# give_back at step 12, projections one step ahead, and three of the scan's sixteen states beside the filter's tail and the value projections

## What is computed

```python
xn = layernorm(x)
# first layer: a state space filter with further small products, and two experts of eight for each sequence
def step(h, t):                       # the scan, 16 states for each of 256 inner channels
    delta_t, B_t, C_t, u_t = t
    h = exp(delta_t * A) * h + delta_t * B_t * u_t
    return h, einsum('bdn,bn->bd', h, C_t)
x = x + filter(xn) + experts(xn)
xn = layernorm(x)
# second layer: causal attention, 16 heads of 64, and two experts of eight for each token
attn = softmax(where(causal, -inf, q @ k.T) / sqrt(64)) @ v
x = x + attn @ wo.T + bo + token_experts(xn)
```

## Time and profile before

| | us |
|---|---|
| three runs | 2887.19, 2894.98, 2903.43; median 2894.98 |
| the profiled execution | 2911.0 |
| its span, first to last instruction | 2909.2 |
| busy: TensorE | 2210.0 (76%) |
| busy: VectorE | 1641.0 (56%) |
| busy: ScalarE | 1182.3 (41%) |
| busy: GpSimd | 956.3 (33%) |
| mean granted clock of TensorE | 0.856 |

### The profile page before, as it was taken

One profiled execution on the slowest core, in us unless ns is written; L12 is line 12 of the kernel. 1 busy time (PEld: TensorE's weight loads), 2 busy tenths in 40 slices (PEclk: granted clock), 3 DMA queues, 4 the chain that ended last, 5 costly groups with the idle time before them and its releaser, 6 DMA issues.

```text
span 2909.2 us, 38779 instructions
## 1 busy us (share of the span) xinstructions
PE 2210.0 (76%) x11640; PEld 1519.0 (52%) x11640; DVE 1641.0 (56%) x2929; ACT 1182.3 (41%) x2702; POOL 956.3 (33%) x581
## 2 busy tenths in 40 slices
PE   3257878877798777976788777887779877788785
PEld 1033556554565545654456545655556555565564
DVE  2953775456754666546765467545675466644231
ACT  2222653434533454334543345333453345423441
POOL 0320661036510563006620176103641057302401
PEclk8577889987899888887899878998799888989897
DMA  2000012211122111211113111221112211131123
GB/s 89 0 15 5 35 67 65 83 52 34 57 89 83 40 47 48 97 65 33 47 60 109 52 38 66 66 83 52 36 55 90 82 40 47 51 122 55 58 73 123
DMA packets 82452, 175.06 MB, mean 60 GB/s; under 512 B 11448, under 2 KB 42560, under 8 KB 81984
## 3 DMA queue, kind: packets, MB, share of 16 engines
q1 hardware_dynamic: 78144, 164.05, 16.8%
q0 software_dynamic: 4096, 8.40, 1.0%
HBM read 123.71 MB, written 15.14 MB: 48 GB/s over the span
## 4 chain that ended last, share of the span: by engine, by line
PE 47%; issue 21%; DVE 11%; POOL 10%; ACT 9%; DMA 2%; SPq 0%; ACTq 0%; POOLq 0%; DVEq 0%
PE G L895 7%; PE G L999 4%; PE G L1014 4%; PE FM L988 4%; POOL REG L1879 3%; POOL YG L1893 3%; PE G L906 2%; PE G L988 2%; DVE HS L1468 2%; PE G L976 2%; PE G L1031 2%; PE FM L718 2%; POOL Y L1868 2%; ACT REG L1258 2%; PE FM L865 1%
## 5 line engine op out<-in xcount | busy, mean ns | idle before, releaser
L1868 POOL TENSOR_TENSOR Y<-Y,HC 128x1024 f32<-128x1024 f32 x128 | 322.9, 2523 | 340.4 <-DVE HC L1480 340.1
L1279 ACT ACTIVATE REG<-G 128x128 f32<-128x128 f32 (+3 forms) x512 | 222.9, 435 | 517.4 <-PE G L999 514.9
L1879 POOL TENSOR_TENSOR REG<-REG,cos_t 128x512 f32<-128x512 f32 x128 | 223.0, 1743 | 570.0 <-ACT REG L1258 569.0
L1014 PE MATMUL G<-REG 128*128 128x64 f32 x2560 | 378.3, 283 | 0.5 <-DVE REG L1761 0.4
L1014 PEld LDWEIGHTS G<-REG 128*128 128x128 f32 x2560 | 364.9, 211 | 1.1 <-issue 0.9
L1468 DVE TENSOR_TENSOR_SCAN HS<-DA,D 128x1024 f32<-128x1024 f32 x128 | 336.1, 2626 | 12.8
L895 PEld LDWEIGHTS G<-XGT,MW 128*128 128x128 f32 x1920 | 296.5, 239 | 57.6 <-issue 57.5
L895 PE MATMUL G<-XGT,MW 128*128 128x128 f32 x1920 | 304.4, 326 | 18.9 <-DMA MW<-moe 18.9
L988 PE MATMUL G<-REG 64*128 64x128 f32 (+3 forms) x768 | 246.5, 536 | 88.8 <-ACT REG L1258 57.7
L988 PE MATMUL FM<-REG 64*128 64x256 f32 (+1 forms) x256 | 143.9, 648 | 175.3 <-ACT EW L1289 65.1
L999 PE MATMUL G<-ident,REG 128*128 128x128 f32 x1280 | 255.3, 302 | 21.1 <-ACT REG L1279 19.1
(11 more groups left out here) (279 smaller groups left out, 3760.0 us busy)
## 6 DMA issues: line engine op xcount, KB each, us to landing
MW<-moe SPq DMA_DIRECT2D x120, 768.0 KB, 4.3
REG<-ROT SPq DMA_DIRECT2D x256, 128.0 KB
EW<-experts SPq DMA_DIRECT2D x16, 514.5 KB, 4.3
XG<-x_rows SPq DMA_DIRECT2D x8, 960.0 KB, 5.6
y_rows<-YO SPq DMA_DIRECT2D x120, 64.0 KB, 1.5
X<-xT SPq DMA_DIRECT2D x8, 256.0 KB, 5.7
W<-weights SPq DMA_DIRECT2D x1, 2048.0 KB, 9.5
REG<-xT SPq DMA_DIRECT2D x8, 256.0 KB, 3.0
```

The source lines that it names most:

```text
L1014: mm = pe.matmul(G[3][:, col:col + DK], PT[:, n % 2, c * P:(c + 1) * P], V[:, c, j * P + h * DK:j * P + (h + 1) * DK], start=c == 0, stop= ...
L1279: act.activation(PT[:, n % 2, 0:width], G[2][:, 0:width], ACT.Copy).then_inc(pt_copy.sem, 1)
L1868: pool.tensor_tensor(Y[:, :, :], Y[:, :, :], HC[:, n % 2, :, :], ALU.add).then_inc(y_add.sem, 1)
L1879: pool.tensor_tensor(rotated, rotated, cos_t[:, :], ALU.mult).then_inc(rope_d.sem, 1)
```

## The change

Three things move; no computation is added or left out.

1. RETURN_STEP goes from 8 to 12, so give_back stands four steps later on TensorE and VectorE. number_places stays in step 9.
2. Project stands in the step before the one that lends its bank, ahead of weigh_values; rotate comes ahead of the two maxima; on ScalarE add_bias, copy_out and rows_turned come right after the step's first copy_turned.
3. States 0 and 1 of the scan are put into phase 1, between filter steps 23 and 28 (kind "s"). State 0 and 1 use the bank FM for B and the place HC_EARLY in REG for HC. State 2 stands in the value stage. The other 13 states are spread over the 32 steps by the table PIECES, about 2.5 steps each. The norms nf and nx use FB alone, so that FC is free for the row of C.

```diff
+        HC_EARLY = REG[:, 14:16, :]
...
+        EARLY = 2
+        EARLY_AT = {23: ((0, 0),), 24: ((0, 1),), 25: ((0, 2), (1, 0)), 26: ((1, 1),), 27: ((1, 2),)}
...
+            PHASE_1 += [("s", piece) for piece in EARLY_AT.get(p, ())]
...
-        PLACE_AT, NUMBER_AT, RETURN_STEP = 2, 9, 8
+        PLACE_AT, NUMBER_AT, RETURN_STEP = 2, 9, 12
...
+        FIRST = EARLY + 1
+        PIECES = {s_: [] for s_ in range(STEPS)}
+        for n_ in range(FIRST, STATES):
+            at_ = (n_ - FIRST) * STEPS / (STATES - FIRST)
+            for part_ in range(3):
+                PIECES[int(at_ + (0.0, 0.7, 1.7)[part_])].append((n_, part_))
...
+            def early_scan(f, n, part, b):
+                if part == 0:
+                    front_b(f, n, b, FM)
+                elif part == 1:
+                    front_c(f, n, b)
...
                 project(b, 1)
-                values_in(b)
+                if f is not None:
+                    front_b(f, EARLY, b)
+                    front_c(f, EARLY, b)
+                values_in(b, f)
...
+                project(b, 2)
                 for s in range(STEPS):
                     j, t_ = s // TILES, s % TILES
                     key = loan[s][0] if s in loan else (None, None)
-                    if key[0] == "proj":
-                        project(b, key[1])
-                    elif key[0] == "out":
+                    following = loan[s + 1][0] if s + 1 in loan else (None, None)
+                    if key[0] == "out":
                         turn_out(b, key[1])
...
                     turn(b, 2 * s + 1)
                     if t_ == 0 and s + 2 < STEPS:
                         scores(b, s + 2)
+                    if following[0] == "proj":
+                        project(b, following[1])
                     weigh_values(b, 2 * s)
...
+                if n == 0 and f is not None:
+
+                    act.wait_ge(y_add.sem, y_add.at(f, EARLY))
...
                 for s in range(STEPS):
                     copy_turned(b, 2 * s)
-                    if f is not None and s % 2 == 0:
-                        front_step(f, s // 2, (1,))
-                    if s + 1 < STEPS:
-                        exponentials(b, 2 * s + 2)
-                    copy_turned(b, 2 * s + 1)
                     key = loan[s][0] if s in loan else (None, None)
                     if key[0] == "proj":
                         add_bias(b, key[1])
...
                     if s + 1 < STEPS:
-                        exponentials(b, 2 * s + 3)
-                    if f is not None and s % 2 and s // 2 + 1 < STATES:
-                        front_step(f, s // 2 + 1, (0,))
+                        exponentials(b, 2 * s + 2, f)
+                    if f is not None:
+                        for n, part in PIECES[s]:
+                            if part == 0:
+                                front_step(f, n, (0,))
+                    copy_turned(b, 2 * s + 1)
+                    if f is not None:
+                        for n, part in PIECES[s]:
+                            if part == 0:
+                                front_step(f, n, (1,))
+                    if s + 1 < STEPS:
+                        exponentials(b, 2 * s + 3, f)
...
                     key = loan[s][0] if s in loan else (None, None)
+                    if key[0] == "proj":
+                        rotate(b, key[1])
                     if s + 1 < STEPS:
                         largest(b, 2 * s + 2)
                         largest(b, 2 * s + 3)
...
-                        if s % 2:
-                            front_step(f, s // 2, 2)
-                        else:
-                            front_step(f, s // 2, 0)
-                            front_step(f, s // 2, 1)
+                        for n, part in PIECES[s]:
+                            front_step(f, n, part)
...
+                    for n in range(EARLY):
+                        front_step(f, n, True)
...
-                    if f is not None and n % 4 == 3:
-                        front_step(f, n // 4)
+                    if f is not None and n % 2:
+                        for k, part in PIECES[s]:
+                            if part == 2:
+                                front_step(f, k)
```

More of the change, by code:

```diff
@@ L530, in each_step @@
                     front_start(f, k, b)
+                if kind == "s" and f is not None:
+                    early_scan(f, k[0], k[1], b)
         @block.sync
@@ L750, in front_b @@
                     if filtered is not None:
-                        pe.wait_ge(nx.s_root.sem, nx.s_root.at(filtered, 1))
-                pe.matmul(FB[:, :], pick[:, n, :], S3[:, :], start=True, stop=True).then_inc(b_mm.sem, 1)
+                        pe.wait_ge(yf_d.sem, yf_d.at(filtered))
+                if filtered is not None and n == EARLY:
+                    pe.wait_ge(xn2_d.sem, xn2_d.at(filtered))
+                pe.matmul(bank[:, :], pick[:, n, :], S3[:, :], start=True, stop=True).then_inc(b_mm.sem, 1)
             def front_c(b, n, filtered=None):
@@ L945, in values_in @@
                         pe.wait_ge(v_copy.sem, v_copy.at(b, n + 1 - len(V_BANK)))
+                    elif n == 2 and f is not None:
+                        pe.wait_ge(db_mul.sem, db_mul.at(f, EARLY))
                     elif n == 3:
@@ L1790, in phase_2 @@
                         largest(b, 2 * s + 3)
+                    if key[0] == "return" and t is not None:
+                        give_back(t, ring_bank[key])
                     if t_ == 0 and j:
                         divide(b, j - 1)
[L1793 to L1796 removed]
                     if s == 1:
@@ L1867, in front_step @@
                 pool.wait_ge(hc_mul.sem, hc_mul.at(b, n + 1))
-                pool.tensor_tensor(Y[:, :, :], Y[:, :, :], HC[:, n % 2, :, :], ALU.add).then_inc(y_add.sem, 1)
+                pool.tensor_tensor(Y[:, :, :], Y[:, :, :], HC_EARLY if early else HC[:, n % 2, :, :], ALU.add).then_inc(y_add.sem, 1)
             def front_end(b):
```

80 lines of the change are left out of this document (50 added, 30 removed).

## The result

The changed kernel takes 2730.8 us (median of four runs, 2729.52 to 2738.27) against 2891.09 (four runs, 2870.63 to 2903.43): ratio 0.946, 95% interval 0.940 to 0.952. The profiled execution took 2738.3 us against 2911.0, 172.7 less; its span is 2736.5. The medians are 160 us apart: the profiled execution of the kernel before was 20 us slower than its median, that of the changed kernel 8.

The account below looks back on a forecast made before the run. No engine is full; hand-over between engines bounds the kernel. Six full laps at -16.5 us (-99), first -15, last -7 make -121 on the profiled 2911.0: 2790, as a median 2775 us; range 2705 to 2870.

Parts of the forecast that it names:

- more comes back: Rival: 24 us of bank waits go, nothing left at number_places, -28 us a lap, median 2695 us; chance 0.15.
- under 15: Sign: TensorE's waits for ScalarE before scores total under 15 us a lap, from 30.8 before.
- the new wait: Sign: TensorE waits before project about 12 us a lap, 0.9 us at each of 13 projections.
- the tail grew: Sign in the filter's tail: XN2 stands 22 to 23 us after the preceding norm's root, before 18.6.
- 16, 3 and 3.5: Savings forecast for a full lap, in us: new order 16, three states out of the steps 3, later give_back 3.5.
- part 2: Three of sixteen scan states leave the attention steps: 3 us a lap saved there, outer bound 6.7.
- The wait before place_i: Sign: VectorE idles 5 to 10 us before the place_i cast, waiting for GpSimd's sum; TensorE feels about 4.
- part 1: Attention steps: projections one step ahead, ScalarE's bias or copy before the exponential; 16 us a lap saved, bounds 0 and 30.8.
- Part 3: give_back at step 12: TensorE's 7.5 us wait goes, number_places waits instead; net -3.5 us, between 0 and -7.5.
- Scans held up by GpSimd: Rival: each of 13 scans may meet a GpSimd add, 9 us a lap, +65, so 2840 us; chance 0.12.
- Project blocking TensorE: Rival: project waits for late exponentials, 3.3 us each, +75, so 2970 us; decides from 2.5 us a projection; chance 0.08.

Follow-up runs that it names:

- e1: Kernel before the change with only give_back moved, from step 8 to step 12; ratio 0.983, 2851 us.
- e3: Kernel before with only the scan's states moved: two into the filter's tail, one into the value stage, thirteen spread over the steps; ratio 0.969, 2816 us.
- e10: Kernel before with decays and norms re-placed and the last three of sixteen states left out, the other thirteen in the old pairs of steps; ratio 0.988, 2857 us.
- e2: Kernel before with only the new order of projections, rotations and ScalarE's bias and copies; states and give_back as before; ratio 0.982, 2847 us.
- e5: Changed kernel with projections, rotations and ScalarE's bias and copies back in the old order; ratio to the kernel before 0.953, 2763 us.
- e4: Changed kernel with give_back put back to step 8; ratio to the kernel before 0.953, 2763 us.
- e7: Changed kernel with GpSimd's sum of the picked rows moved ahead of the weights of the rows; ratio to the kernel before 0.930, 2695 us.
- e12: Changed kernel with no early states: all sixteen in the steps, D and scan in different steps; ratio to the kernel before 0.954, 2766 us.
- e8: Changed kernel with project at its old place on TensorE, VectorE and ScalarE keeping the new order; ratio to the kernel before 0.935, 2712 us.

## Why the prediction came out as it did

The time, 2731 us, lies in the range (2705 to 2870) and 44 below the forecast, 4 outside the forecast's own band (2735 to 2815); it stands between the forecast and the rival "more comes back" (2695). The terms against the two profiles, the stretches cut at the first and last exponential and at XN2 (rounded):

| | forecast, us | measured |
|---|---|---|
| steps, six full laps | -135 | -164 |
| steps, first lap | -19 | -20 |
| steps, last lap | -7 | -19 |
| phase 1, the tail in it | +26 | +23 |
| value stages | +14 | +9 |
| the rest | 0 | -1 |
| all | -121 | -173 |

**Right: the mechanisms and their places.** Scores no longer wait for lent banks (1.3 us, "under 15"), project has the new wait (14.9, forecast 12), give_back waits for nothing, the sum is waited for before place_i instead, and the tail grew to 22.8 us (forecast 22 to 23). The idle time of the full lap fell by 22.5 us (22.3 in the mean), as 16, 3 and 3.5 make; that it agrees so well is in part luck, as part 2 below shows. The wait before place_i was 3.7 us (5.1 in one of the six laps) where 5 to 10 was expected. The agreement of phase 1 (+26 and +23) is partly luck as well, since its laps come in two lengths, as the last section shows.

**Mis-sized: what a wait is worth.** The terms counted idle time alone. I named the clock (0.84) only in favour of a rival, and gave it no term. Busy time fell by 5.0 us a full lap in the mean, 30 over six, which is the whole difference between -135 and -164; in the last, idle fell by 12.7 where 7 was forecast, and busy by 6.4 more. e1 shows the second at its cleanest: a wait of 6.3 us removed, 13.6 gained in the last lap; in its full laps busy time went the other way.

**Failed: who removes the bank waits.** Part 2 said: "What it costs the steps is the difference of the two laps", and set 3 us a lap with 6.7 as the outer bound; e3 measured 17.4 (mean of six laps, 173.5 to 156.1). A lap with scans against one without tells only what the states' number costs, and that price held: 0.98 a state forecast, 1.2 in e10. It says nothing of a new spacing of the same work. D and scan apart take many of the waits that part 1 had claimed for itself: in e3, without part 1, they fell from 30.8 to 20.6 us. In turn part 1's 16 us came out as 8.6 alone (e2, 173.5 to 164.9) and 1.1 on top of the rest (e5, 147.2 to 146.1). The sum was near because both parts reach for one pot, which I counted once; the shares inside were wrong.

**Part 3** forecast -3.5 a lap. Against e4 idle time fell by 3.9 in the mean, and the steps by 1.7 (147.8 to 146.1), since busy time rose by 2.2. The wait before place_i, which I priced at the 4 us of idle time that TensorE feels, has a price in busy time too: in e7, where it is shorter, busy time is 5.2 us less.

**The rivals.** Scans held up by GpSimd: in the steps of the six full laps the mean went from 2.51 to 2.86 us, 0.34 for each of 13, 4.5 us a lap on VectorE where 9 was feared. In e12, with sixteen, it is 3.29. The rows at 1938 us show it from both sides: the scan was 0.73 longer after 0.86 of overlap with L1936, and L1939 ended some 1.1 after the scan did. The Trainium skill, page "SBUF — State Buffer", section "SBUF: two separate sides", has VectorE with two inputs in SBUF and GpSimd exclude each other on a shared port pair. By that rule the trace agrees. Project blocking TensorE: real, 1.24 us each where 2.5 would decide, and e8 shows that the kernel is 1.1% better without it. So the sign of that rival was right for project's place on TensorE and wrong for the order as a whole.

Open is why busy time is longer with project ahead: e5 and e8, both without it, need 116.2 and 119.3 us in the mean against 123.5 (granted clock 0.92, 0.88 and 0.87), and in the changed kernel the fall in steps 10 and 11 comes with waits of 1.78 and 2.11 us before project. No run holds the waits fixed and moves only the clock.

## What to carry to other kernels

Price a wait of TensorE with the busy time behind it: read the granted clock stretch by stretch, and compare the busy time of the same matmuls, not only the gaps. Do it over all laps: the lap looked at first can be the one that shows most. Nor is the sign given: in e7 and in the last lap of e1 busy time fell with the idle time, but in the full laps of e1, and from e4 and e5 to the changed kernel, it rose while idle time fell. Where two edits reach for the same waits, count the waits once and expect either alone to take many of them. A difference between a stage with a piece of work and one without prices its number; how it is bunched on an in-order queue, ahead of what others wait for, is a term of its own and may be the larger.
